# A pair's two shift products on partitions 0-1 and 64-65 in place of 0-3 for both

## The reference

```python
def mha(xq, ctx, wq, wk, wv, wo, bo):
    q = (xq @ wq).reshape(b, sq, H, DH).transpose(0, 2, 1, 3)
    k = (ctx @ wk).reshape(b, sk, H, DH).transpose(0, 2, 1, 3)
    v = (ctx @ wv).reshape(b, sk, H, DH).transpose(0, 2, 1, 3)
    scores = jnp.einsum('bhqd,bhkd->bhqk', q, k) / math.sqrt(DH)
    attn = jax.nn.softmax(scores, axis=-1)
    ...
h1 = adaln(x, t, norm1_w, norm1_b)
x = mha(h1, h1, attn1_wq, attn1_wk, attn1_wv, attn1_wo, attn1_bo) + x
h2 = adaln(x, t, norm2_w, norm2_b)
x = mha(h2, context, attn2_wq, attn2_wk, attn2_wv, attn2_wo, attn2_bo) + x
h3 = adaln(x, t, norm3_w, norm3_b)
x = glu_ff(h3, ff_w1, ff_b1, ff_w2, ff_b2) + x
```

## Time and profile before

| | |
|---|---|
| median of 3 runs | 4336.03 us |
| lowest, highest | 4332.26, 4339.48 us |
| the profiled execution's own time | 4336.59 us |
| its span, first to last instruction | 4334.8 us |
| mean clock granted to TensorE | 0.960 |
| the stage of the change | about 2290 to 2763 us of the span |

### The profile page before, as it was taken

The page is one execution under the profiler, slowest core; times in us unless marked ns, Lnnn a source line. Parts: engine busy times, 40 slices in busy tenths (PEclk is TensorE's granted clock), DMA queues, the critical chain, the costliest instruction groups (busy, mean ns, idle before and its releaser), DMA issues. The chain is left out here.

```text
span 4334.8 us, 67854 instructions
## 1 busy us (share of the span) xinstructions
PE 3659.7 (84%) x19196; PEld 2057.9 (47%) x19196; DVE 2698.2 (62%) x13488; ACT 2307.6 (53%) x6608; POOL 661.0 (15%) x2307
## 2 busy tenths in 40 slices
PE   7888888888888888888799999779898989898978
PEld 2356666666676666666533334322223232323222
DVE  3457777777777777777644454538575766666634
ACT  4456666666666666666543334216564646464633
POOL 0222222222222222222240000300001010101002
PEclk8999999999999999999999999759999999999979
DMA  0100000000000000000101000011111121212100
GB/s 10 59 1 1 1 1 2 2 1 2 2 1 1 2 1 2 2 1 2 37 1 39 1 1 1 23 60 47 61 47 60 47 67 40 80 32 73 30 20 5
DMA packets 48774, 93.57 MB, mean 22 GB/s; under 512 B 11296, under 2 KB 31792, under 8 KB 48144
## 3 DMA queue, kind: packets, MB, share of 16 engines
q1 hardware_dynamic: 48400, 89.22, 6.4%
HBM read 72.88 MB, written 15.39 MB: 20 GB/s over the span
## 5 line engine op out<-in xcount | busy, mean ns | idle before, releaser
L923 PE MATMUL ps<-g_dh,w_p 128*128 128x77 f32 x2032 | 453.0, 304 | 342.9 <-DVE g_dh L1014 342.9
L931 PE MATMUL ps<-g_dh,w_p 128*128 128x128 f32 x4064 | 662.6, 285 | 0.0
L2362 ACT ACTIVATE t_ex<-ps 128x1024 f32<-128x1024 f32 (+1 forms) x480 | 479.0, 1021 | 306.9 <-PE ps L2305 295.9
L2451 DVE TENSOR_REDUCE t_ncol<-ps 128x1 f32<-128x512 f32 x768 | 502.6, 684 | 115.4 <-PE ps L2279 110.4
L923 PEld LDWEIGHTS ps<-g_dh,w_p 128*128 128x128 f32 x2032 | 302.1, 188 | 537.4 <-DVE g_dh L1014 537.4
L988 DVE SCALAR_TENSOR_TENSOR g_used<-g_encg,g_e 128x77 f32<-128x77 f32 x3072 | 550.7, 229 | 0.0
L931 PEld LDWEIGHTS ps<-g_dh,w_p 128*128 128x128 f32 x4064 | 535.1, 191 | 0.0
L958 ACT ACTIVATE g_th<-ps 128x77 f32<-128x77 f32 x1024 | 242.4, 237 | 401.8 <-PE ps L923 401.8
L940 PE MATMUL ps<-g_th,g_vrep 128*128 128x77 f32 x2048 | 453.8, 303 | 0.0
L935 PE MATMUL ps<-g_dh,g_uhh 128*128 128x129 f32 x2032 | 437.0, 297 | 0.0
L997 DVE TENSOR_REDUCE g_ntop<-ps 128x1 f32<-128x77 f32 x1024 | 244.0, 238 | 259.0 <-PE ps L940 211.0
(11 more groups left out here) (481 smaller groups left out, 5423.3 us busy)
## 6 DMA issues: line engine op xcount, KB each, us to landing
t_qst<-t_turn_q SPq DMA_DIRECT2D x288, 96.0 KB
t_kst<-t_turn_k SPq DMA_DIRECT2D x144, 96.0 KB
t_turn_q<-t_part SPq DMA_DIRECT2D x24, 384.0 KB, 2.9
t_turn_k<-t_part SPq DMA_DIRECT2D x12, 384.0 KB, 2.6
t_wf<-in_t_wf SPq DMA_DIRECT2D x6, 514.5 KB, 5.4
m_experts<-in_experts SPq DMA_DIRECT2D x1, 3072.0 KB, 12.2
t_wa<-in_t_wa SPq DMA_DIRECT2D x6, 448.0 KB, 3.4
t_wx<-in_t_wx SPq DMA_DIRECT2D x6, 448.0 KB, 4.1
```

Source lines behind the costliest of these rows:

```text
L923: M(att[c], w["att_h"], moved(c, t, S), start=False, stop=True, skip_group_check=True).then_inc(*st.sem("att", c))
L931: return M(gates[c][:, g], w["uh"][:, g * D:(g + 1) * D], moved(c, t, SPAN), start=False, stop=False, skip_group_check=True)
L2362: A(ex[0:kw, slot[pf, c, l, n]], ps[0:kw, at:at + 2], ACT.Exp, scale=SCALE).then_inc(*st[c].sem(f"{pf}e{n}"))
L2451: V.tensor_reduce(ncol[:, c, n % TT, n // TT:n // TT + 1], ps[:, at], AX, ALU.max, negate=True)\
```

## The change

The weights of the shift products become a 128 x 128 tile of bf16 ones (`onesb`), and the shift rows of head h stand on partitions 64h (high) and 64h + 1 (low). For that `nb` has, for each head, 64 columns, of which the first two hold the high and low parts and the rest zero, filled once at the stage's start; the transposes of line 1440 take 66 of these 128 columns and give 66 rows, and `row` has 66 partitions, of which 2 to 63 are zero and aren't read. Each shift product takes two rows, of partitions 0-1 or 64-65. The number and order of products is the same.

```diff
--- before.py
+++ after.py
@@ -1297,15 +1297,16 @@
 
         hn = sb("h", [P, B, T])
         center, identb = sb("center", [P, P]), sb("identb", [P, P], BF16)
-        pick, sel = sb("pick", [4, 2]), sb("sel", [4, 2, P], BF16)
+        onesb = sb("onesb", [P, P], BF16)
         W = {"s": sb("ws", [P, PAIRS2, 4 * P]), "x": sb("wx", [P, PAIRS2, 4 * P])}
 
         qh = {"s": sb("qs", [P, NR, T]), "x": sb("qx", [P, NR, T])}
         kh = {"s": sb("ks", [P, NR, T]), "x": sb("kx", [P, NR, S])}
         va = {"s": sb("vs", [P, NR, TT, P]), "x": sb("vx", [P, NR, 1, P])}
         ncol = {"s": sb("ns", [P, NR, TT, 2]), "x": sb("nx", [P, NR, TT, 2])}
-        nb = {"s": sb("nbs", [P, NR, TT, 4], BF16), "x": sb("nbx", [P, NR, TT, 4], BF16)}
-        row = {"s": sb("rs", [4, NR, T], BF16), "x": sb("rx", [4, NR, T], BF16)}
+        nb = {"s": sb("nbs", [P, NR, TT, 2, DH2], BF16), "x": sb("nbx", [P, NR, TT, 2, DH2], BF16)}
+        RW = DH2 + 2
+        row = {"s": sb("rs", [RW, NR, T], BF16), "x": sb("rx", [RW, NR, T], BF16)}
         ex = sb("ex", [P, EXR, 2, T])
 
         added = sb("added", [P, 2, T])
@@ -1437,7 +1438,8 @@
                 elif what == "th":
                     pe.wait_ge(*done("lo", of, u))
                     for t in range(TT):
-                        mm = M(ps[0:4, at, t * P:(t + 1) * P], nb[of][:, r, t], identb[:], start=True, stop=True)
+                        mm = M(ps[0:RW, at, t * P:(t + 1) * P], nb[of][:, r, t].rearrange("p h n -> p (h n)")[:, 0:RW], identb[:],
+                               start=True, stop=True)
                     mm.then_inc(*signal("th", of, u))
                 elif what == "b":
                     if n == 0:
@@ -1447,7 +1449,8 @@
                         d = slice(DH2 * h, DH2 * h + DH2)
                         M(ps[0:kw, at + h], kh[of][d, r, n * P:n * P + kw], qh[of][d, r], start=True, stop=False)
                     for h in range(2):
-                        mm = M(ps[0:kw, at + h], sel[:, h, 0:kw], row[of][:, r], start=False, stop=True)
+                        hl = slice(DH2 * h, DH2 * h + 2)
+                        mm = M(ps[0:kw, at + h], onesb[hl, 0:kw], row[of][hl, r], start=False, stop=True)
                     mm.then_inc(*signal("b", of, u, n))
                 elif what == "tot":
                     pe.wait_ge(*done("ad", of, u, TT - 2))
@@ -1548,11 +1551,10 @@
             V = nc.vector
             V.tensor_copy(identb[:], k.ident[:]).then_inc(filled, 1)
             V.tensor_tensor(center[:], k.ident[:], k.mean_w[:], ALU.subtract).then_inc(filled, 1)
-            V.tensor_tensor(pick[:], k.ident[0:4, 0:2], k.ident[0:4, 2:4], ALU.add).then_inc(filled, 1)
-            dve.wait_ge(filled, 3)
-            for h in range(2):
-                fill = V.tensor_scalar(sel[:, h], k.ones[0:4, :], pick[:, h:h + 1], None, ALU.mult)
-            fill.then_inc(filled, 1)
+            V.tensor_copy(onesb[:], k.ones[:]).then_inc(filled, 1)
+            V.memset(nb["s"][:], 0.0)
+            V.memset(nb["x"][:], 0.0).then_inc(filled, 1)
+            dve.wait_ge(filled, 4)
             for what, of, u, n in program("dve"):
                 r = u % NR
                 if what == "norm":
@@ -1583,12 +1585,12 @@
                             .then_inc(*signal("m", of, u, n))
                 elif what == "hl":
                     dve.wait_ge(*done("m", of, u, NKT[of] - 1))
-                    V.tensor_copy(nb[of][:, r, :, 0:2], ncol[of][:, r]).then_inc(*signal("hi", of, u))
+                    V.tensor_copy(nb[of][:, r, :, :, 0], ncol[of][:, r]).then_inc(*signal("hi", of, u))
                     dve.wait_ge(*done("hi", of, u))
-                    V.tensor_tensor(nb[of][:, r, :, 2:4], ncol[of][:, r], nb[of][:, r, :, 0:2], ALU.subtract).then_inc(*signal("lo", of, u))
+                    V.tensor_tensor(nb[of][:, r, :, :, 1], ncol[of][:, r], nb[of][:, r, :, :, 0], ALU.subtract).then_inc(*signal("lo", of, u))
                 elif what == "rc":
                     dve.wait_ge(*done("th", of, u))
-                    V.tensor_copy(row[of][:, r], ps[0:4, place["th", of, u, 0]]).then_inc(*signal("rc", of, u))
+                    V.tensor_copy(row[of][:, r], ps[0:RW, place["th", of, u, 0]]).then_inc(*signal("rc", of, u))
                 elif what == "ad":
 
                     if n == 0:
```

## The result

| | before | change |
|---|---|---|
| median (runs) | 4331.48 us (8) | 4307.34 us (8) |
| lowest run | 4324.38 | 4297.05 |
| the profiled execution's span | 4334.8 | 4297.4 |
| mean clock granted to TensorE in it | 0.960 | 0.964 |

A forecast was written before the change was run, and what follows sets the result against it. TensorE, busy all the time in the edited stage, was taken to set the pace. Terms of -11.2 - 0.6 - 3.5 + 0.3 + 0.9 = -14.1 us took the median 4336.03 to 4322 us, range 4316.5 to 4330.

The forecast's parts named there:

- What bounds the stage: Edited transformer block: TensorE sets the pace, busy 260.00 of 260.00 us in self-attention and 109.85 of 110.00 in cross-attention.
- 0.216 us a step from the overlap: Shift products of line 1450: second starts 0.007 us after the first, not 0.223; 80 steps, at most 17.3 us.
- 12 steps held back by the copy: Self-attention steps where TensorE waits for VectorE's copy L1591 of the shift rows: gain 0.05 us each, 0.6 in all.
- Transposes +0.3 us: Transposes of line 1440 load 66 columns of weights in place of 4: 32 x 0.01 = 0.3 us added, bounds 0 and 12.5.
- Fills +0.9 us: VectorE's constants at the stage's start: a cast and two zero fills of 0.71 us each, net +0.9, bounds -0.5 and +2.4.
- The stage's sum, -14.1: Changed stage, gains and costs together: -11.2 - 0.6 - 3.5 + 0.3 + 0.9 = -14.1 us.
- from the stage to the whole: Whole kernel: the stage's -14.1 us taken off 4336.59 gives 4322.5, and by the median 4321.9, said as 4322.
- The base: Whole kernel before the change: median of three runs, 4336.03 us, from which the forecast was reckoned.
- the rivals: Pair overlaps but freed time becomes waits, 15%, 4330; products still serial, 8%, 4337.2; second waits for emptied array, 5%, 4344.6.

## Why the prediction was right or wrong

- *What bounds the stage* (TensorE, always busy): right. It stayed so; windows of the change show 255.2 of 256 us and 95.0 of 95.
- *0.216 us a step from the overlap*: right; 0.213 was measured where no copy is waited for. 15.4 us between the stretches with and without it, 15.3 in the sum. The 0.007 us of the score products' row was the right neighbour (0.003 was measured), and so was the form in the last stage.
- *12 steps held back by the copy*: right, mis-sized a little: they gained 0.08 each instead of 0.05.
- *Transposes +0.3 us*: **wrong in sign**, -3.1. I compared four narrow products with four wide ones by their own length, 0.39 against 0.40, and did not look at the distance ahead of them. The Trainium skill's page "TensorEngine Tiling (Array Packing)", section "Key Properties", which I had applied to the rows of weights only, says that changing the tiling mode drains TensorE. The same page's section "Available Configurations" in the Trainium skill lists the modes by rows and columns, with 128, 64 or 32 columns. The trace agrees if the shape of the weights picks the mode: 0.52 us into 4 columns behind 128 and 0.43 into 66, and on the way out 0.149 us from 4 to 128 columns, 0.056 from 66 to 128, and 0.149 from either to 64.
- *Fills +0.9 us*: nearly right, +1.2, since one fill starts 0.81 us after the other and not 0.71. *The clock after them*: not in the sum. It took 1.2 to 3.0 us in the three profiles of the change; of the kernel before three profiles show nothing and one 2.0 us.
- *The stage's sum, -14.1*: -14.2, -16.0 and -14.2 in the three profiles: right, partly by errors that happen to cancel.
- **The step that failed is the last one: from the stage to the whole.** "Other stages vary, so a median can be off by about 2 us on its own," says the prediction. I had every stage but the changed one at no change, with 2 us for scatter. In its place the runs show a stage that takes another time when what runs ahead of it is shifted: the ternary stage took 86 to 90 us in three profiles of the change and 94 and 102 in two of the kernel before, with the same code, and a pause of 1.3 us moved it by 14 and the median by 11. By the mean of these profiles it gives 9.5 us; with 14.8 in the changed stage that is 24.3, where the medians have 24.1. So close an agreement is luck: the profiled executions have means of 4331.8 and 4300.0 us, 31.8 apart, of which the other stages have 7.5. Firmer is the run with the pause: with the ternary stage at 103.2 it is 13.6 us below the kernel before, and the changed stage less the pause gives 14.8 - 1.3 = 13.5. I had a chance of 0.73 on faster by over 0.2%, which was right, and a lower end that allowed no gain outside the stage. The spans of other stages were in the trace that I had.
- *The base*: 4336.03 from three runs was 4.5 us above the median of eight, more than the 2 us allowed. Without that the forecast would have been about 4317.4, and 4307.3 would still be 10 us below it.
- None of the rivals came true. The pair does start together, and little of it turned into waits.

Open is what in the clock's history makes 86 or 103 us, and with it how often each occurs in a kernel; the traces show when the clock fell, not why. The distance of 0.318 us behind a shift pair is not open: it is 0.216 where the products on both sides have 64 rows.

## What to carry to other kernels

Two short products of different data cost little more than one if they stand on different partitions (here they also go to different banks of PSUM, which was not varied); read the neighbouring rows for a pair that does so already, and then look at what surrounds a product, since the shape of its weights, against that of its neighbours, goes with the distance to them: giving the shift products the 64 rows of the score products, most of them zero, was worth 10.6 us of the stretch, without one instruction more. And where a later stage runs at a clock that rises and falls, a change of some us ahead of it can be worth several times its size (here 11 us lost for 1.3): compare stage by stage, and test with a pause, before a whole-kernel difference is put down to the edit.

## What the runs showed of the hardware that I had not expected

- Products with 4 columns of weights behind ones with 128: 0.52 us from the last start to theirs; with 66 columns 0.43. Products with 128 columns behind them: 0.149 us against 0.056; products with 64 columns: 0.149 behind either.
- Products of 2 or 4 rows behind ones of 64 rows: 0.52 us; of 64 rows, 0.42. Products of 64 rows behind an overlapping pair: 0.318 us from the start of a pair of 2 rows, 0.216 from one of 64; products of 128 rows: 0.318 and 0.312.
- Beside GpSimd's fill of 1.38 us VectorE's cast took 1.42 us in place of 0.23; beside one of 0.76 us, in the run with wide transposes, 0.80.
- The same stage with the same code took 85.8 to 103.2 us; TensorE was busy for 53.7 of the one and 73.4 of the other, at a mean clock of 0.68 and 0.54, and VectorE, ScalarE and GpSimd about as long in both.
